# Fused attend-and-route stage: expert choice over two steps, a tile's shift made in the step of its statistics

## What is computed

```python
x = x + _layernorm(attention(_layernorm(x)))   # random-feature linear attention, 16 heads, 128 features
x = x + _layernorm(ffn(_layernorm(x)))         # 32 experts, top 4, capacity 512, and a shared expert
...
S = jnp.einsum('chlm,chld->chmd', k_phi, v);  sum_k = jnp.sum(k_phi, axis=2)
numer = jnp.einsum('chlm,chmd->chld', q_phi, S)
denom = jnp.maximum(jnp.einsum('chlm,chm->chl', q_phi, sum_k), EPS)
out = (numer / denom[..., None]) ... @ w_out.T
...
scores = jax.nn.sigmoid(X @ gate_w.T)
_, idx = jax.lax.top_k(scores + bias[None, :], K)
w = take(scores, idx);  w = w / sum(w)
pos = running count of the tokens that chose the same expert, in order of tokens;  valid = pos < C
```

## Time and profile before

| | us |
|---|---|
| median of 3 runs | 2157.99 |
| lowest, highest run | 2147.43, 2160.95 |
| profiled execution | 2154.41 |
| its span | 2152.6 |

### The profile page before, as it was taken

The page is one execution under the profiler, slowest core; times in us unless marked ns, Lnnn a source line. Parts: engine busy times, 40 slices in busy tenths (PEclk is TensorE's granted clock), DMA queues, the critical chain, the costliest instruction groups (busy, mean ns, idle before and its releaser), DMA issues. The chain is left out here.

```text
span 2152.6 us, 33711 instructions
## 1 busy us (share of the span) xinstructions
PE 1828.6 (85%) x12976; PEld 890.7 (41%) x12976; DVE 1205.9 (56%) x2230; ACT 1124.9 (52%) x1371; POOL 772.0 (36%) x718
## 2 busy tenths in 40 slices
PE   8899999999979999799888898404999988987995
PEld 6444444444427877133333333202444444433342
DVE  7676667666650000158878888831444434435887
ACT  5564555545425665577777776402444444432443
POOL 0000000000000000025677788874777777751110
PEclk9999999999989999899999999756999999998998
DMA  7435353546238886578777875322789999876994
GB/s 257 144 123 187 108 200 106 163 148 211 90 113 220 212 211 160 131 182 238 217 213 221 249 219 169 137 72 90 168 194 267 250 257 227 176 138 169 352 343 155
DMA packets 187791, 403.05 MB, mean 187 GB/s; under 512 B 33780, under 2 KB 72052, under 8 KB 171008
## 3 DMA queue, kind: packets, MB, share of 16 engines
q1 hardware_dynamic: 83184, 222.41, 35.2%
q10 hardware_dynamic: 67584, 122.17, 16.3%
q0 software_dynamic: 36864, 56.32, 13.7%
HBM read 237.06 MB, written 174.98 MB: 191 GB/s over the span
## 5 line engine op out<-in xcount | busy, mean ns | idle before, releaser
L258 PE MATMUL s_proj<-s_xT,keep_wqkv 128*128 128x512 f16 x1536 | 341.8, 379 | 0.0
L1271 POOL DMA_INDIRECT slot_dram<-s_filled,s_slots x256 | 305.2, 1192 | 95.1 <-issue 72.9
L1415 POOL DMA_INDIRECT acc_dram<-s_y,s_slot x128 | 205.9, 1609 | 101.3 <-DMA acc_dram<-s_y,s_slot 47.1
L906 PE MATMUL s_y<-keep_wo,s_at_hl 128*128 128x512 f16 x768 | 194.7, 408 | 42.6 <-ACT s_z L997 42.6
L258 PEld LDWEIGHTS s_proj<-s_xT,keep_wqkv 128*128 128x128 f16 x1536 | 147.8, 98 | 183.2 <-issue 12.6
L237 PE MATMUL s_proj<-keep_wqkv,s_xT 128*128 128x512 f16 x768 | 179.7, 393 | 34.5 <-ACT s_xT L500 34.5
L1522 ACT ACTIVATE s_gate<-s_gates 128x512 f32<-128x512 f32 x96 | 57.3, 597 | 281.2 <-PE s_ups L1474 219.1
L339 POOL TENSOR_SCALAR s_rstd<-s_mv 128x4 f32<-128x4 f32 x16 | 16.0, 998 | 496.5 <-DVE s_mv L354 496.5
L518 ACT ACTIVATE s_hl<-s_rot 128x1024 f16<-128x1024 f32 x64 | 67.6, 1057 | 221.1 <-DVE s_rot L400 220.6
L1577 DVE SCALAR_TENSOR_TENSOR s_h<-s_gate,s_ups 128x512 f32<-128x512 f32 x96 | 65.9, 686 | 199.0 <-ACT s_gate L1522 199.0
L676 ACT ACTIVATE s_phi<-s_logits 128x1024 f32<-128x1024 f32 x128 | 131.1, 1024 | 84.5 <-PE s_logits L697 84.5
(11 more groups left out here) (164 smaller groups left out, 3217.0 us busy)
## 6 DMA issues: line engine op xcount, KB each, us to landing
s_x<-x_in SPq DMA_DIRECT2D x32, 1024.0 KB, 9.8
qk_dram<-s_hl ACTq DMA_DIRECT2D x32, 1024.0 KB
keep_ahead<-qk_dram SPq DMA_DIRECT2D x48, 512.0 KB
acc_dram<-s_zero SPq DMA_DIRECT2D x17, 1024.0 KB, 11.5
v_dram<-s_v ACTq DMA_DIRECT2D x16, 1056.0 KB, 5.8
s_v<-v_dram SPq DMA_DIRECT2D x16, 1056.0 KB
s_spread<-share_dram SPq DMA_DIRECT2D x64, 256.0 KB, 4.6
x_dram<-s_x ACTq DMA_DIRECT2D x16, 1024.0 KB, 4.9
```

The source lines that it names most:

```text
L258: mm = nc.tensor.matmul(out[:, 512 * b:512 * b + 512], left, right, start=(c == 0 and i == 0), stop=(c == EC - 1 and i == 2))
L906: mm = nc.tensor.matmul(y[m % 2][:], at_hl[n % 2][:, s, c, a * P:(a + 1) * P], keep["wo"][:, w, c, :], start=(c == 0 and i == 0), stop=(c ...
L1271: nc.gpsimd.indirect_dma_start(out=io["slot"], out_offset=bass.IndirectOffsetOnAxis(ap=slots[n % 2][:, a * K + j:a * K + j + 1], axis=0), ...
L1415: nc.gpsimd.indirect_dma_start(out=io["acc"], out_offset=bass.IndirectOffsetOnAxis(ap=slot[e % RING][:, a, 0:1], axis=0), in_=y[e % 2][:, ...
```

## The change

The choice of the experts is cut in two functions. `rank` (scores, bias, maxima) stays in the step with lag 18; `choose` (indices, one-hot, mask) is done with lag 19. The count of places on PE and `weigh` on DVE move to lag 20, so the position is read with lag 21. PE waits for the read position before the fourth tile's gates instead of the third's. `make_shift` is taken from the head of a step, where it served the tile measured one step before, and put behind `divide`, `make_at_low` and `weigh` of the step in which the tile was measured. `make_share`, `rank`, `choose` and `fill` come after it.

The order on DVE after the change: `read_total` (0), `read_position` (1), `make_low`, `add`, `measure_y`, `measure_x1`, `aggregate(s - 9)`, `divide` (2), `make_at_low` (3), `weigh` (0), `make_shift(s - 9)`, `make_share` (0), `rank` (2), `choose` (3), `fill` (1).

```diff
-        SCORE, CHOOSE, PLACE, WEIGH, FILL, SEND = 18, 18, 19, 19, 21, 21
+        SCORE, RANK, CHOOSE, PLACE, WEIGH, FILL, SEND = 18, 18, 19, 20, 20, 21, 21
...
-                    if a == 2:
+                    if a == A - 1:
                         pe.wait_ge(where_ready, n)
...
-            def choose(n):
+            def rank(n):
                 dve.wait_ge(score_ready, n + 1)
...
                     ins = nc.vector.max(top[:, a, :], biased[:, a, :])
                 then(ins)
+
+            def choose(n):
                 for a in range(A):
...
-                if 0 <= s - SCALE < UNITS:
-                    make_shift(s - SCALE)
                 n = group_at(s, PLACE + 1)
...
-                n = group_at(s, A)
-                if n is not None:
-                    make_share(n)
                 n = group_at(s, A + 2)
                 if n is not None:
                     divide(n)
                 n = group_at(s, A + 3)
                 if n is not None:
                     make_at_low(n)
+                n = group_at(s, WEIGH)
+                if n is not None:
+                    weigh(n)
+                if 0 <= s - MEASURE < UNITS:
+                    make_shift(s - MEASURE)
+                n = group_at(s, A)
+                if n is not None:
+                    make_share(n)
+                n = group_at(s, RANK)
+                if n is not None:
+                    rank(n)
                 n = group_at(s, CHOOSE)
                 if n is not None:
                     choose(n)
-                n = group_at(s, WEIGH)
-                if n is not None:
-                    weigh(n)
```

## The result

The changed kernel takes 2229.39 us (median of 4 runs, 2227.53 to 2235.35), the kernel before 2154.57 us (4 runs, 2147.43 to 2160.95): a ratio of 1.0328, with a 95% interval of 1.0287 to 1.037. By the ratio it is slower by about 71 us; the two medians lie 75 us apart. The prediction had the direction and the engine right. It said 2204 us, with a range of 2168 to 2228: the measured median is 1.4 us above the top of that range, and the loss was half as large again as its +47.

What follows compares the result with a forecast made beforehand. POOL was taken to bound the fused stage's groups. At 34.2 us a group the intervals give +41.4, the first choice +1.5, two disturbances +4: total +46.9, forecast 2204 us, range 2168 to 2228.

Steps and rivals of the forecast that it cites:

- What bounds the kernel before: Fused stage: POOL sets the pace, 24.0 us of own work in a measured group of 29.6 us.
- The split: Choice in two steps on DVE: work only moves between steps, sum over the group 0; most waits for dens go.
- The ring: Step 1: POOL's first send waits for fill, fill for the shift, the shift for POOL's rstd; +4.0 us per group.
- The stretching of the sends: POOL's sends lengthened by DVE's instructions: 5.6 us a group, bounds 3.2 and 7.
- the hand schedule: One group followed through POOL and DVE from rstd of step 1: 34.6 us.
- the lock: Port shared by POOL and DVE: the larger part if the sum of POOL's sends falls by more than 40 us.
- the sentence on PE's `count`: PE's count moved past a step, 14 small matmuls: cost 0, with 3.6 us to spare per group.
- (a): Rival: waiting DVE leaves the port free for POOL's sends, stretching under 2.7 us a group, 2123 us; chance 0.07.
- (c): Rival: PE's granted clock falls to 0.7, its 26 us become 37, +36 us on top, 2240 us; chance 0.05.
- No earlier start helps: Step 1: the idle time before POOL's first send stays, since POOL, DVE and POOL wait for each other.

Runs made afterwards that it cites:

- e6: The kernel before with two of each tile's four sends on POOL left out; 2099.99 us.
- e1: The changed kernel with make_shift put back at the head of the next step, the choice over two steps kept; 2159.29 us.
- e2: The kernel before with only make_shift moved into the step of its statistics, the choice left in one step; 2228.45 us.
- e4: The changed kernel with read_total moved from the head of step 0 to the end of step 3, behind the shift and ahead of choose; 2203.94 us.
- e9: The changed kernel with twelve useless matmuls added on PE in every step 0, in front of the sum that waits for den; 2212.95 us.
- e8: The changed kernel with read_total ahead of choose in step 3 and fill ahead of the shift in step 1; 2169.51 us.
- e10: The changed kernel with read_position moved from the head of step 1 to just ahead of fill; 2206.74 us.

## Why the prediction was right or wrong

**What bounds the kernel before: right.** POOL's full group of 29.6 us was the basis. e6 supports it: with half of POOL's sends the groups take 28.9 us in place of 30.7.

**The split costs and brings nothing in the sum: right for the split alone** (e1), but for a reason that was missed. The waits for `dens` shrank less than expected, and a wait for the position appeared.

**The ring, +4.0 us a group: right in place and size.** The idleness is 4.2 to 4.4 us in fourteen groups, against 4.2 worked out; a fifteenth wait has 0.30. The prediction asked for 13 or more, over 45 us in total; it is 59.5. DVE's waits for `rstd` were to exceed 80 us and are 89.9. The move of the shift alone (e2) gives the whole loss.

**The stretching of the sends: of the right kind, too large by 0.7 us a group.** The prediction took 34.2 us for the ring, the hand schedule gave 34.6; where nothing else disturbs it (e4) it is 33.4 to 33.5. That is 24.0 + 4.0 + 0.66 of waiting for the statistics of step 0 + 4.7 to 4.8 of stretching. The hand schedule is too long in step 2: its own terms, a first send at 4.2, four sends of 1.27 and 1.6 for `divide`, end at 10.9 and not at 11.7, and in the trace of e4 these sends end at 10.4. The mean of a send fell from 1192 to 1096 ns, while that of POOL's add of eps rose from 287 to 710 ns. Before, and after:

```profile
L1271 POOL DMA_INDIRECT slot_dram<-s_filled,s_slots x256 | 305.2, 1192 | 95.1 <-issue 72.9 <-DVE s_slots L1205 17.0 <-DVE s_shift L1125 3.0
...
L1262 POOL TENSOR_TENSOR s_rstd<-s_mv,s_eps 128x2 f32<-128x2 f32 x54 | 15.5, 287 | 10.9 <-DVE s_mv L1150 10.3
```

```profile
L1276 POOL DMA_INDIRECT slot_dram<-s_filled,s_slots x248 | 271.7, 1096 | 130.2 <-issue 68.6 <-DVE s_slots L1207 59.5 <-ACT s_z L997 1.8
L1269 POOL TENSOR_TENSOR s_rstd<-s_rstd,s_power 128x2 f32<-128x2 f32 x54 | 38.9, 720 | 4.2
L1267 POOL TENSOR_TENSOR s_rstd<-s_mv,s_eps 128x2 f32<-128x2 f32 x54 | 38.4, 710 | 47.9 <-DVE s_mv L1150 47.5
```

The second view ends before the last eight sends; all 256 take 279.5 us. That is 26 us less than 305.2, under the 40 that would have made the lock the larger part. `make_at_low` now falls on the add rather than on a send (2.12 us at 1197.96), as the hand schedule assumed; `divide` still holds a send, 1.97 us at 1188.62.

Two small slips in the prediction change nothing: 2201.3 and 3.6 make 2204.9, and the send at 1285.09 ends 0.86 us after `divide`, not 0.84.

**The step that failed** is the sentence on PE's `count`: "still behind the mask by the same distance; PE has 3.6 us to spare per group: 0". The distance to the mask was the wrong thing to compare. `read_position` moved to the head of step 1, directly ahead of the statistics that close the ring, and what it waits for is PE's whole step 0. That step starts when PE gets `den`. PE's waits of `y` for `z` fell from 42.6 to 26.8 us, while its stops of `total` for `den` rose from 5.9 to 29.4; a wait took the place of the one removed. DVE waits 36.2 us for the position. Where nothing else disturbs the groups this costs 3.4 us in each, the difference between 36.9 and 33.5, and 25 us of the time by e4, the whole of what the prediction was short of. Without it the changed kernel takes 2203.94 us, where the prediction had 2204. That the two agree so closely is partly luck, since an over-sized stretching made up for one disturbed group. Why PE's results come as late as they do is only in part known (e9).

**The rivals.** (a), with the port left free, did not come: the stretching was 4.7 us and not under 2.7. (c), the clock, was part of it. It was priced as a fall over the whole group, to 0.7, and its sign was to be a group over 36 us with a clock under 0.75. The groups are that long (36.9), but their mean clock is 0.86; what mattered was the place of the fall, behind PE's stop and ahead of the position. The prediction compared PE's 26 us of work with the length of a group, while the wait was set within one step of it.

**"No earlier start helps"** was too strong. Of the 49 us that e4 still loses, e8 wins back 34 by the order of `fill` and shift inside step 1 alone, so that order is worth most of the ring.

## What to carry to other kernels

When a consumer is moved up to the step of its producer, ask what the producer's engine must finish first, and what stands behind the consumer that this same engine waits for. Here that closed a ring between two full engines, and each turn of it was paid in idleness. An engine that is relieved of one wait runs ahead to its next one, so look up what that next stop delays, and in which step, not whether the engine has time to spare over a whole group. Put waits on other engines behind the work that others are waiting for (e10 did only this and won 23 us).

## What the runs showed of the hardware

The idle time of POOL between the end of an input on DVE and an indirect DMA that was already waiting for it is 0.78 us before the change. After it, `slots` at 1184.76 takes 0.17 us and the send starts at 1185.71, again 0.78. A send that does not wait starts 0.20 to 0.30 us after its predecessor. So a wait for data in front of such a DMA costs half a microsecond more than the lateness itself.

PE's records and its releases disagree in the slow steps. The records of the matmuls for the position end by 1210.7 and those of the first logits of step 1 by 1211.1, but the instructions that wait for them, on DVE and on ACT, start at 1214.38 and 1214.43 with no other releaser. This happened in nine groups of the changed kernel, and in e9 with the granted clock at 1.00 in the stretch.

The records are the less steady of the two. In six groups in a row (those of the changed kernel with `total` restarting from 1056.96 to 1241.39) the copy of the position starts 9.84 to 9.93 us after PE restarts `total`, while the last record of `count` starts anywhere from 5.98 to 7.34 us after it. At a granted clock of 1.00 in e9 the same matmuls take 4.57 us in the records (1200.39 to 1204.96). Twice that is 9.1 us, an estimate of the time at the lower level, so a slow stretch that is longer than the records show would come near to the 9.9. Against it stands e9, where the copy comes 6.9 to 8.2 us after the restart of `total` with a recorded clock of 1.00 in the group read. What holds the release back is not shown by these runs.
